# Forty late scatters that each wait for the landing of the one before

## The reference

```
x = x + attention(layernorm(x))      # 16 heads of 8 features, 4 key/value heads,
                                     # rms norm of q and k, rotary positions, gain,
                                     # causal window of 32, heads mixed in pairs, Wo
x = x + moe(layernorm(x))            # router: 8 experts, the two best of each token with
                                     # masked-softmax weights w1, w2;
                                     # out = w1*E1(x) + w2*E2(x),
                                     # E(x) = (silu(x @ gate.T) * (x @ up.T)) @ down.T, width 256
```

## Time and profile before

| | |
|---|---|
| median of 3 runs | 562.23 us (561.99 to 567.3) |
| profiled execution, span | 673.3 us (no time around the span is shown) |
| PE busy | 550.8 us (82%) |
| DVE busy | 424.6 us (63%) |
| ACT busy | 370.5 us (55%) |
| POOL busy | 345.8 us (51%) |
| scatters (L1297), 128 | 126.9 us, 992 ns each |
| gathers (L1368), 128 | 122.3 us, 955 ns each |
| mean granted TensorE clock | 0.918 of full |

### The profile page before, as it was taken

One profiled execution on the slowest core, in us unless ns is written; L12 is line 12 of the kernel. 1 busy time (PEld: TensorE's weight loads), 2 busy tenths in 40 slices (PEclk: granted clock), 3 DMA queues, 4 the chain that ended last, 5 costly groups with the idle time before them and its releaser, 6 DMA issues.

```text
span 673.3 us, 23426 instructions
## 1 busy us (share of the span) xinstructions
PE 550.8 (82%) x7519; PEld 473.6 (70%) x7519; DVE 424.6 (63%) x1700; ACT 370.5 (55%) x1170; POOL 345.8 (51%) x536
## 2 busy tenths in 40 slices
PE   3899999999999999987657669888887878887860
PEld 1578887777878777875537569777787778776850
DVE  5788898898989988883554226355444454544452
ACT  4467776666757766651246437455554555554530
POOL 3333346667776666763343381435455444556355
PEclk9999999999999999995756779899899899999895
DMA  7333333233332222222111223334444443443333
GB/s 215 67 72 74 71 81 96 65 82 82 69 72 46 53 45 53 53 48 62 33 54 44 65 67 96 99 114 135 115 120 126 111 123 102 126 122 107 103 107 82
DMA packets 126310, 58.20 MB, mean 86 GB/s; under 512 B 54000, under 2 KB 121712, under 8 KB 126192
## 3 DMA queue, kind: packets, MB, share of 16 engines
q1 hardware_dynamic: 117424, 39.03, 23.3%
q0 software_dynamic: 8192, 16.79, 8.6%
q10 hardware_dynamic: 576, 0.88, 0.4%
HBM read 28.15 MB, written 24.58 MB: 78 GB/s over the span
## 4 chain that ended last, share of the span: by engine, by line
PE 69%; another core or an unknown queue 9%; issue 8%; ACT 5%; DMA 3%; DVE 2%; POOL 2%; SPq 1%; ACTq 1%; POOLq 0%; DVEq 0%
PE chb L727 16%; PE pv L581 7%; PE chb L639 6%; PE pm L592 5%; PE pp L752 5%; PE pp L661 5%; PE pv L752 4%; PE chb L630 4%; PE chb L626 3%; PE tp L744 2%; PE tp L684 2%; POOL ga L1368 2%; PE tp L554 2%; PE tp L560 2%
## 5 line engine op out<-in xcount | busy, mean ns | idle before, releaser
L1368 POOL DMA_INDIRECT ga<-expert_out,row_all x128 | 122.3, 955 | 137.1 <-DVE yb L1257 83.9
L1297 POOL DMA_INDIRECT expert_in<-xn,slot_r x128 | 126.9, 992 | 121.5 <-DVE slot_r L921 96.5
L727 PE MATMUL chb<-xbT,wcur 128*128 128x128 f32 x1144 | 162.4, 288 | 0.0
L727 PEld LDWEIGHTS chb<-xbT,wcur 128*128 128x128 f32 x1144 | 150.6, 205 | 0.0
L1250 DVE TENSOR_TENSOR hT<-sil,chb 128x256 f32<-128x256 f32 x143 | 60.1, 420 | 114.2 <-ACT sil L507 86.3
L507 ACT ACTIVATE sil<-chb 128x256 f32<-128x256 f32 x143 | 54.9, 384 | 124.2 <-PE chb L727 57.2
L417 ACT ACTIVATE pT<-chb 128x512 f32<-128x512 f32 x128 | 77.1, 602 | 69.8 <-PE chb L639 59.5
L938 DVE TENSOR_REDUCE mx<-chb 128x8 f32<-128x512 f32 x128 | 86.7, 685 | 18.0 <-PE chb L639 13.9
L524 ACT COPY wcur<-wgu 128x512 f32 x143 | 89.9, 629 | 5.6 <-issue 5.3
L744 PE MATMUL tp<-ident,xb 128*128 128x128 f32 x143 | 42.5, 297 | 48.9 <-issue 38.6
L581 PEld LDWEIGHTS pv<-vext,pT 128*64 128x64 f32 x1984 | 68.1, 140 | 13.8 <-issue 13.3
(11 more groups left out here) (140 smaller groups left out, 1051.1 us busy)
## 6 DMA issues: line engine op xcount, KB each, us to landing
xb<-expert_in SPq DMA_DIRECT2D x143, 64.0 KB
expert_out<-yb SPq DMA_DIRECT2D x71, 128.0 KB
xa<-x SPq DMA_DIRECT2D x16, 256.0 KB
out<-oo SPq DMA_DIRECT2D x31, 128.0 KB
qk<-qk SPq DMA_DIRECT2D x64, 48.0 KB
wgu<-w_gu SPq DMA_DIRECT2D x16, 128.0 KB
expert_in<-xn,slot_r POOLq DMA_INDIRECT x128
ga<-expert_out,row_all POOLq DMA_INDIRECT x128
```

The lines of the kernel that those rows point to most:

```text
L727: last = nc.tensor.matmul(chb[:, b % 4, n * P:(n + 1) * P], wcur[:, b % 3, n * P:(n + 1) * P], xbT[:, b % 4, :], start=True, stop=True)
L1297: nc.gpsimd.indirect_dma_start(xs_dram, bass.IndirectOffsetOnAxis(ap=slot_r[:, q % 4, 2 * v + k:2 * v + k + 1], axis=0), xn2[:, t % 16, :] ...
L1368: nc.gpsimd.indirect_dma_start(ga[:, q % 2 * TPS + v, j, :], None, ys_dram[0:min(blocks, LIVE) * P, :], bass.IndirectOffsetOnAxis(ap=row_a ...
```

## The change

`scatter` gets a condition: for tiles whose scatter falls in a step past the last rotation step (`t + 20 >= 64`, tiles 44 to 63), POOL first waits until the scatter issued before this one has landed in full. `one_landed(n)` finds the semaphore of scatter `n` (they are numbered `2 * t + k`, eight to a group, four semaphores in turn) and the count that it has then.

```diff
+            def one_landed(n):
+
+                pool.wait_ge(scat[n // (2 * TPS) % 4], (n // (8 * TPS) * 2 * TPS + n % (2 * TPS) + 1) * 16)
+
             def scatter(t, k):
                 q, v = t // TPS, t % TPS
+                if t + L_SCAT - L_RMS >= NT:
+                    one_landed(2 * t + k - 1)
                 nc.gpsimd.indirect_dma_start(
                     xs_dram, bass.IndirectOffsetOnAxis(ap=slot_r[:, q % 4, 2 * v + k:2 * v + k + 1], axis=0),
                     xn2[:, t % 16, :], None).then_inc(scat[q % 4], 16)
```

## The result

The changed kernel takes 591.17 us (median of 4 runs, 589.78 to 592.08), the kernel before 563.11 us on the same chip: ratio 1.0486, 95% interval 1.0446 to 1.0527. The profiled execution of the changed kernel took 592.08 us, 0.9 over its median, so its trace stands for the timed runs. That of the kernel before doesn't (span 673.3 us); the same kernel was therefore recorded once more, and that recording ("before again", span 565.7 us) is what the trace after is compared with.

The account below looks back on a forecast made before the run. TensorE was taken to bound the kernel's middle, GpSimd only its end. The 562.2 us median plus 25 for the late first combine plus 4 for half clock gave 591 us, range 570 to 625.

Parts of the forecast that it names:

- The chain without pause: GpSimd's late scatters: the groups join into one chain, 95.6 us to the last start; first gather waits only for GpSimd.
- The cadence, 2.45 us: Each late scatter on GpSimd: landing 2.15 plus release 0.30 us instead of 1.26 us spacing; ends 2.20 and 3.20.
- From the last scatter to the first combine: Chain's tail: `rows(0)` end 9.3, first gather 0.3, its partner 1.3, landing 2.4, combine 0.1 us.
- When the first combine is wanted, T + 84: VectorE's first combine in timed runs: 84 us after T, the first late scatter; upper end 93; so 25 us late.
- The clock, +4, and nothing won back: TensorE after its stop: half clock costs 4 us (bounds 2 and 7); none of the 25 us is regained.
- The late start of the first loads: SP's first expert block loads start 5 us later; not added, because the longer chain holds the combine.
- The recorded span, 647 us: Profiled execution after the change: about 647 us, shorter by 30 less 4 if thin scatters make no holes.
- the rule of tracing: Tracing block pushes back rather than lose records, so holes belong to the recording: 591 us with this rule, 536 without.
- (a): Rival, faster: bursts' holes are in timed runs too and vanish with the change; 536 us, chance 0.18.
- (b): Rival, no change: scatters land sooner unrecorded, cadence under 1.81 us, chain in time; 562 to 567 us, chance 0.14.
- (c): Rival, more: each wait costs release 0.80 plus landing 2.40, 3.20 us; about 620 us; chance 0.68 together with the forecast's chain.

Follow-up runs that it names:

- Experiments 4: Changed kernel with the landing waits kept only for tiles 48 to 63 (32 of 40 scatters): 584.35 us, ratio 1.0375 to the kernel before.
- 6: Changed kernel, all 40 waits, but scatters of tiles 56 to 63 issued behind `rows(0)`, one ahead of each of the first sixteen gather pairs: 571.21 us, ratio 1.0136.
- 9: Changed kernel, all 40 waits, with the seven operations of `rows(0)` put between the last group's scatters: 586.74 us, ratio 1.0390 to the kernel before.
- experiment 12: Kernel before, no landing waits, `rows(0)` held back until the 24th `yb` copy, testing its collision with VectorE's places(1): 563.76 us, ratio 1.0003.
- experiment 2: Changed kernel with the landing waits kept only for tiles 44 to 47 (8 scatters of 40): 565.78 us, ratio 1.0045 to the kernel before.
- experiment 1: Kernel before, unedited, recorded a second time: 562.90 us, ratio 0.9992, span 565.7 us.
- the pairs: Changed kernel where only the first scatter of each late tile waits (20 of 40 waits), two under way at a time: 559.80 us, ratio 0.9954.

## Why the prediction was right, and where it wasn't

Forecast 591 us, measured 591.17. The mechanism is the one forecast, step by step; part of the closeness is luck, since three terms were off and their errors cancelled.

- **The chain without pause.** Right: 38 waits in the trace, the groups joined into one, the first gather behind `rows(0)` alone. That the last scatter is at 397.72, where 397 was forecast, is luck: T is 14.7 us earlier than in the recording that the forecast counts from, and the chain 16.4 longer. TensorE isn't at work throughout it, as forecast, but stops at 383.82. Experiments 4, 6 and 9 bear out that the chain's end is what counts: 7.7 us off its front bring 6.8 us (591.17 to 584.35), 6.6 off its tail about one per cent.
- **The cadence, 2.45 us.** Mis-sized. Undisturbed it is 2.49 to 2.50 (landing 2.21 to 2.24 where I took 2.15, release 0.27 where I took 0.30), but the mean is 111.95 / 39 = 2.87: 22 of the 39 spacings lie in the forecast 2.4 to 2.6, eight between 3.06 and 4.89. What goes with the long ones is less SP's transfers than a piece of the queue that the profile calls instruction. The DMA queues in a spacing of 3.75 us (316.9 to 320.6) and in one of 2.50 (328.2 to 330.6):

```profile
q1 hardware_dynamic: 543, 0.25, 23.6%
q0 software_dynamic: 32, 0.07, 6.2%
q8 instruction: 1, 0.02, 2.3%
...
q1 hardware_dynamic: 415, 0.20, 28.1%
q0 software_dynamic: 32, 0.07, 8.6%
```

  Ten spacings with the scatter's own packets alone take 2.49 us in mean, twelve with SP's beside them 2.65 (at most 2.93), eleven with a 16 KB piece of q8 3.51, and six with the smaller q14 instead 2.78. The eleven hold 11 of the 15 us over 39 x 2.49. No run took these pieces away, so their part isn't shown beyond that; and 1.6 of those 11 us, in the longest spacing (4.89), are a pause of GpSimd's own, which the same scatter has before again. Start of the last scatter at T + 111.95 instead of T + 95.6. I had taken the best case of the two rows for all 39.
- **From the last scatter to the first combine.** 13.7 us (411.38 - 397.72) against 13.4: right.
- **When the first combine is wanted, T + 84.** Mis-sized: T + 94.1, over my upper end of 93. I had worked it out by taking holes from a disturbed recording, and counted as holes some of what the slots lose of their own: before again they lose 13.5 us over 1.45 a slot in that stretch, the collision of experiment 12 among them, where I had left 5.1. It is 10 us in the kernel's favour, against 16.4 of the cadence: late by 31.5 instead of 25.
- **The clock, +4, and nothing won back.** The half clock came: granted 0.50 until 417.50, 4.4 us from TensorE's first matmul at 413.11, some 2 us of it lost. But "nothing of the 25 is won back, because TensorE has no slack in the slots that follow" was wrong. The sixteen combines that follow have 6.2 us of slack before again (52.6 for 32 slots, of 46.4), and 1.6 after. Net it is -4.3 where I put +4.
- **The late start of the first loads.** Right that the whole change covers it, T + 25.9 against T + 22.4 for the first transpose (3.5 us, where I had put 5); alone it costs 0.45% (experiment 2). The cost of nothing held only beside the longer chain.
- **The recorded span, 647 us, and the rule of tracing.** Wrong: 590.3. The side forecast took the holes to be part of every recording. The Trainium skill, "NOTIFIC — the notification-queue block", section 7.1, has the block push back rather than lose a record; two spans of one kernel, 673.3 and 565.7, show that recording as such needn't hold the engines. It gave 591 for another reason than the one that holds: not that recordings have holes and timed runs none, but that one execution had them. Whether its recording had a part in them isn't shown.
- **Rivals.** (a) fell with experiment 1. (b) needed 1.81 us a scatter, from a combine wanted at 84; with T + 94.1 that bound is (94.1 - 13.7) / 39 = 2.06. Undisturbed a scatter takes 2.49, and the pairs' 1.95, under the bound, cost nothing. (c), 3.20 each, was passed by seven single spacings, not by the mean.

## What to carry to other kernels

A wait for the previous landing turns an issue interval (1.26 us here) into a round trip (2.87), and what it costs is read at the first consumer queued behind the whole chain: the chain's end, less the time at which that consumer is wanted. Let two be under way and the cost is gone, or put the consumer ahead of the tail of the chain and three quarters of it are. Before taking terms from a recording whose span is 20% over the timed median, record the kernel again, and cost a chain by the mean of its link beside the real traffic, not by its best case.

## What the runs showed of the hardware

- **VectorE stands while a GpSimd operation reads SBUF.** A TENSOR_SCALAR of 0.18 us took 4.01, a SCALAR_TENSOR_TENSOR on one column 3.45 instead of 0.16, each ending with GpSimd's TENSOR_TENSOR beside it; `hT`, with one operand in PSUM, kept its 0.41 us beside GpSimd's next ones. The Trainium skill, "SBUF — State Buffer", section "Who interferes with whom", has it so: GpSimd shares a port pair with VectorE; a VectorE operation in a two-port mode contends for it, one with two inputs in SBUF does against a GpSimd operation that reads SBUF, and the loser blocks fully. The rows agree on who is caught. By the same section of the Trainium skill whoever issues first keeps the pair; here the record of the TENSOR_SCALAR begins 0.51 us before that of GpSimd's operation (351.07 and 351.58), and it is the one that lasts, which no run here explains.
- **An indirect scatter's landing is 2.21 to 2.24 us when alone**, on top of which the waiting queue starts 0.27 later. The long ones, up to 3.9 us, came with a piece of the instruction queue in the transfers (the eleven such spacings are 3.51 us in mean, the twelve with SP's transfers alone 2.65). The chain shows one:

```profile
381.21 3.79 DMA expert_in<-xn,slot_r
385.00 0.27 issue
```

- **Executions of one program can differ by a hundred microseconds in the recording**: 673.3 and 565.7, with holes of 9 to 12 us in the one, in which every compute engine but GpSimd stood, and none in the other. I couldn't find the cause.
